# The experts' second weight matrices: loaded tile by tile into three buffers, in place of all eight kept in SBUF

## The chip, the cores and the metric

The kernel runs on one core of one Trainium2 chip. The metric is the device time of one execution in microseconds. The kernel is one launch: everything from the input x to the output is computed in it.

## What is computed

The reference is a small audio tower on x of shape (8, 128, 256): a token stage (smoothing in time and a projection to 256 features), attention, a mixture of experts, a second attention with a sigmoid-exponential weight, and a feed-forward layer with values rounded to eight bits. There are 8 x 256 = 2048 tokens of 256 features. The change concerns the mixture of experts, which is this:

```python
logits = x_flat @ gate_w.T + gate_b
probs = jax.nn.softmax(logits * ROUTE_SCALE, axis=-1)
topk_vals, topk_idx = jax.lax.top_k(probs, TOPK)          # TOPK = 2 of E = 8
dense_gate = jnp.zeros((N, E), probs.dtype).at[jnp.arange(N)[:, None], topk_idx].set(topk_vals)
h = jax.nn.relu(jnp.einsum('nd,edh->neh', x_flat, w1) + b1)     # w1: (8, 256, 1024)
y = jnp.einsum('neh,eho->neo', h, w2) + b2                      # w2: (8, 1024, 256)
out_flat = jnp.einsum('ne,neo->no', dense_gate, y)
```

Both weight matrices of one expert hold 1 MB each, in float32.

## The kernel before

The program is a row of blocks; within a block each engine has its own instruction list, written out by hand, and semaphores order the engines. The queues that matter are SP's, which issues nearly all DMAs in the order of its list and waits in that list, and PE's. Nothing is planned by a compiler: what stands behind a wait in SP's list is issued after it.

**First block (token stage, first attention, gate).** It works on the 8 batches in a software pipeline (`batches`, `iteration(b, u, k)`). For each batch SP issues twelve DMAs of 128 KB that spread parts of q and k over the partitions (`spread`, line 451), one small DMA (line 469) and the load of x of a later batch (line 400). Between them stand the loads of the eight second matrices (`load_w2`, line 436): experts 0, 4 and 5 at b = 0, experts 1 to 3 at b = 1 together with the biases (`load_b2`, line 440), and experts 6 and 7 after the last batch. They all go to `w2s`, 64 KB of each partition. GpSimd scatters each token's normalised row to the list `xg` in DRAM of each of its two experts. At the end of the block the kernel counts the tokens of each expert and makes a table `tile_e` with the expert of each of 39 tiles of 128 token slots, and `tile_row` with the tile's place in `xg`. SP then writes zeros behind the lists (line 385), and issues the first expert load `load_w1(sp, 0)` (line 370) and the first tile of rows `load_tile(sp, 0)` (line 376).

**Second block (experts, second attention).** `moe_tiles` runs `tile(i, u)` for i from -3 to 38 on every engine. In step i PE does the first layer of tile i+1 (line 1623), the transposes of the rows of tile i+2 (line 1637) and the second layer of tile i (line 1657). ACT and DVE each take half of the ReLU (lines 1248 and 1451), and DVE adds the bias and gives the result in `yt` (line 1458). SP in step i loads the rows of tile i+3 (line 376, two buffers `xt_in`) and its first matrix (line 370, three buffers `w1b`), then waits for `yt` of tile i and stores it to `yg` in DRAM (line 1142). Loads whose expert is known only at run time first read the table with `value_load`. PE also reads `tile_e`, once for each tile, to find the second matrix in `w2s`; it does so just ahead of the second layer.

Some steps carry work of the next stage: in steps 22 to 28 PE makes q, k and v of batch 0 of the second attention, and SP issues the twelve spreads of that batch (line 1128), three in step 26, three in 27, four in 28 and two in 29, each group right behind the store of `yt`. GpSimd gathers rows of `yg` back (`gather`, line 1188) once 16 tiles are stored, and again once 32 are.

The last block holds the feed-forward layer of the second half. The lists before the change, as far as the diff touches them:

Of the kernel before, what the change touches and what calls it, by code (L numbers as in the profile page):

```python
# [22 lines left out]
F32 = mybir.dt.float32  # L23
# [8 lines left out]
P = 128  # L32
# [64 lines left out]
def tower_kernel(nc, a, out):  # L97
    with ExitStack() as ctx:
# [72 lines left out]
        def carve(shape, dt, size):  # L171
            n = size
            for s in shape:
                n *= s
            start = used[0]
            used[0] = start + (n + 31) // 32 * 32
            assert used[0] <= ARENA, used[0]
            v = arena[:, start:start + n].bitcast(dt)
            if len(shape) == 2:
                v = v.rearrange("p (a b) -> p a b", a=shape[0])  # L180
            if len(shape) == 3:
                v = v.rearrange("p (a b c) -> p a b c", a=shape[0], b=shape[1])
            if len(shape) == 4:
                v = v.rearrange("p (a b c d) -> p a b c d", a=shape[0], b=shape[1], c=shape[2])
            return v


        b2r = carve([EXPERTS, D], F32, 4)
        w2s = carve([EXPERTS, HC, D], F32, 4)


        used[0] = B2_BYTES + W2_BYTES
# [130 lines left out]
            w8_in w8_step w8_mm w8_done q_step am_mm b_parts qz_q fT_mm fT_done f_mm f_o f_out""".split()  # L323
        scat = [sem(f"scat{u}") for u in range(2)]
        x_ld = [sem(f"x_ld{u}") for u in range(2)]
        w1_ld = [sem(f"w1_ld{n}") for n in range(W1_BUFS)]
        y_st = [sem(f"y_st{u}") for u in range(2)]
        o_out = [sem(f"o_out{u}") for u in range(2)]
# [28 lines left out]
        def batches(eng, iteration):  # L357

            for b in range(-2, 2):
                iteration(b, b % 2, b // 2)  # L360
            with eng.Fori(0, (B - 4) // 2) as it:
                for u in range(2):
                    iteration(it * 2 + (2 + u), u, it + 1)
            for b in range(B - 2, B + 2):
                iteration(b, b % 2, b // 2)

        def load_w1(sp, i):

# [24 lines left out]
        with nc.Block() as block:  # L393

            @block.sync
            def _(sp):
# [34 lines left out]
                            sp.dma_start(cols[:, i, j:j + 1], a[name][j * P:(j + 1) * P].rearrange("(h d o) -> d h o", h=HALVES, o=1)  # L431
                                         ).then_inc(S["w_in"], 16)

                def load_w2(e):

                    sp.dma_start(w2s[:, e], a["L0_ffn_w2"][e].rearrange("(c p) n -> p c n", p=P)).then_inc(S["w_exp"], 16)

                def load_b2():

                    sp.dma_start(b2r, a["L0_ffn_b2"].rearrange("(o e) d -> o e d", o=1).to_broadcast([P, EXPERTS, D])  # L440
# [13 lines left out]
                def iteration(b, u, k):  # L454
                    if stages(b + 2, 2, LAST):
                        load_x(b + 2, u, k + 1)
                    if isinstance(b, int) and b == 0:
                        load_w2(0)
                        load_w2(4)
                        load_w2(5)  # L460
                    if isinstance(b, int) and b == 1:
                        sp.wait_ge(S["wT_mm"], WT_STEPS)
                        for e in range(1, 4):
                            load_w2(e)
                        load_b2()
                    if stages(b, 0, LAST):

                        sp.wait_ge(S["mT_done"], b + 1)
                        sp.dma_start(stackq[SHIFT_ROW:SHIFT_ROW + 1, u], mT[0:HEADS, :]).then_inc(S["mrow"], 16)
                    if stages(b + 1, 0, LAST):  # L470
                        v = 1 - u
                        spread(b + 1, v, 0, 0, S["qh_done"], S["stk_q"])
                        spread(b + 1, v, 0, 1, S["kh_done"], S["stk_k"])
                        spread(b + 1, v, 1, 0, S["qm_done"], S["stk_q"])
                        spread(b + 1, v, 1, 1, S["km_done"], S["stk_k"])
                        spread(b + 1, v, 2, 0, S["ql_done"], S["stk_q"])
                        spread(b + 1, v, 2, 1, S["kl_done"], S["stk_k"])
# [2 lines left out]


                sp.wait_ge(S["xT_mm"], B)
                load_w2(6)
                sp.wait_ge(S["v_mm"], B)
                sp.wait_ge(S["stk_q"], 16 * SLOTS6 * B)
                sp.wait_ge(S["stk_k"], 16 * SLOTS6 * B)
                load_w2(7)
                zero_tails(sp, range(0, EXPERTS, 2))
                sp.wait_ge(S["p_step"], TILE_E_STEP)
                load_w1(sp, 0)  # L490
                sp.wait_ge(S["zfill"], 16 * (EXPERTS + 1))
                for u in range(2):
                    sp.wait_ge(scat[u], 16 + 16 * TOPK * QT * B // 2)
# [623 lines left out]
        with nc.Block() as block:  # L1117
            @block.sync
            def _(sp):
                def spread(b, u, part, which, done, landed):  # L1120

                    sp.wait_ge(done, b + 1)
                    if part == 0 and which == 0:
                        settled(sp)
                        wait(sp, S["s2_mm"], PAIRS * (b - 1))
                    stack = (stackq1, stackk1)[which]
                    for slot in (Q_SLOTS, K_SLOTS)[which][part]:
                        sp.dma_start(stack[u][DH * slot:DH * (slot + 1)].rearrange("d h t -> d (h t)"),
                                     n_qkp[which][:, part].rearrange("p j t -> p (j t)")).then_inc(landed, 16)

                def tile(i, u):
                    if i == 2:
                        sp.dma_start(w8, a["L1_ffn_weight"].rearrange("(j p) i -> p j i", p=P)).then_inc(S["w8_in"], 16)
                    v = 1 - u
                    if has(i + 3) and i + 3 >= 1:
                        wait(sp, S["tx_mm"], i + 2)
                        load_tile(sp, i + 3)
                        wait(sp, S["l1_hi"], i + 4 - W1_BUFS)
                        load_w1(sp, i + 3)
                    if has(i):  # L1140
                        sp.wait_ge(S["y_ev"], i + 1)
                        sp.dma_start(yg[i * P:(i + 1) * P, :], yt[:, u]).then_inc(y_st[u], 16)
                    if i == 26:
                        spread(0, 0, 0, 0, S["n_qh"], S["n_stkq"])
                    if i == 27:
                        spread(0, 0, 0, 1, S["n_kh"], S["n_stkk"])
                    if i == 28:
                        spread(0, 0, 1, 0, S["n_qm"], S["n_stkq"])
                        spread(0, 0, 1, 1, S["n_km"], S["n_stkk"])
                    if i == 29:  # L1150
                        spread(0, 0, 2, 0, S["n_ql"], S["n_stkq"])
                        spread(0, 0, 2, 1, S["n_kl"], S["n_stkk"])

                moe_tiles(tile)


                def iteration(b, u, k):
                    if stages(b + 1, 0, LAST):
                        spread(b + 1, 1 - u, 0, 0, S["n_qh"], S["n_stkq"])
                        spread(b + 1, 1 - u, 0, 1, S["n_kh"], S["n_stkk"])  # L1160
                        spread(b + 1, 1 - u, 1, 0, S["n_qm"], S["n_stkq"])
                        spread(b + 1, 1 - u, 1, 1, S["n_km"], S["n_stkk"])
                        spread(b + 1, 1 - u, 2, 0, S["n_ql"], S["n_stkq"])
                        spread(b + 1, 1 - u, 2, 1, S["n_kl"], S["n_stkk"])

                all_batches(iteration)
# [393 lines left out]
            def _(pe):  # L1560
# [69 lines left out]
                def tile(i, u):  # L1630
# [8 lines left out]
                    if has(i):  # L1639
                        if i == W8_TILE + 1:  # L1640
                            pe.wait_ge(S["w8_step"], 1)
                            pe.transpose(w8_am, w8s[:, 0:1].to_broadcast([P, P]), ident[:]).then_inc(S["w8_mm"], 1)
                        if i == W8_TILE + 4:
                            pe.wait_ge(S["w8_step"], W8_STEPS)
                            for c in range(DC):
                                for j in range(DC):
                                    mm = pe.transpose(w8_turn[:, c * D + j * P:c * D + (j + 1) * P],
                                                      w8q[:, j, c * P:(c + 1) * P], identb[:])
                            mm.then_inc(S["w8_mm"], 1)
                        if i == 0:  # L1650
                            pe.wait_ge(S["w_exp"], 16 * (EXPERTS + 1))
                        e = pe.value_load(tile_e[0:1, i:i + 1], min_val=0, max_val=EXPERTS - 1)
                        pe.wait_ge(S["reluA"], i + 1)
                        pe.wait_ge(S["reluD"], i + 1)
                        wait(pe, S["y_ev"], i)
                        for c in range(HC):
                            mm = pe.matmul(y_bank, hidT[:, u, c, :],  # L1657
                                           w2s[:, one(e), c, :].rearrange("p o n -> p (o n)"), start=(c == 0), stop=(c == HC - 1))
                        mm.then_inc(S["l2_mm"], 1)
                    if i == 22:  # L1660
                        turned_input(0)
# [226 lines left out]
```

## Time and profile before

| | us |
|---|---|
| median of 3 runs | 851.28 |
| lowest and highest | 846.99, 853.36 |
| the profiled execution | 855.8 |
| its span, first to last instruction | 854.0 |

The profile is that of one execution, on one core. Busy times are those of an engine's instructions; a matmul's end is modelled, and matmuls overlap their weight loads (PEld). The granted clock is TensorE's, as a share of full speed. The DMA share is the mean busy share of the core's 16 DMA engines and can pass 1 where packets overlap. "To landing" is the time from the issue of a DMA to the arrival of its last byte. A span cut into 40 slices gives 21.35 us for each. SP, ACT and POOL rows with a q are rows of that engine's DMA queue: when the instruction was issued, and for how long the issue took, not how long the data moved.

### The profile page before, as it was taken

To read this page: it belongs to the slowest core of one execution; us is meant where nothing else is said; L and a number is where in the kernel's file an instruction comes from. 1 tells how busy PE (TensorE), PEld (TensorE's weight loads), DVE (VectorE), ACT (ScalarE), POOL (GpSimd) and SP (SyncE) were. 2 spreads that over 40 slices of the span, in tenths; PEclk is the share of its full clock that TensorE was granted. 3 is DMA by queue.
4 is the path that set the end of the run, shared out by engine and by line. 5 is a ranking of instruction groups with operands and counts; after the bars stand their busy time and mean duration, and the time that the engine had idled before them with its cause. 6 is when DMAs were issued, how large, how long until landed. Compare 5 with 4: busy or idle time off the path is not lost. (4 is left out here: it accounts for less than half of the span.)

```text
span 854.0 us, 15973 instructions
## 1 busy us (share of the span) xinstructions
PE 730.1 (85%) x5604; PEld 580.3 (68%) x5604; DVE 447.0 (52%) x1111; ACT 349.9 (41%) x596; POOL 121.7 (14%) x166
## 2 busy tenths in 40 slices
PE   6488989889886299999999999998589888898646
PEld 5367767767664199999999999997366555664312
DVE  4536776776465222333223132231667888766677
ACT  3143345325432022222222132223687888988513
POOL 2010131232123300000010000101332223100000
PEclk9799999999999599999999999999798988998855
DMA  7989366346541555555565559740764466642002
GB/s 178 206 127 211 45 84 81 64 65 87 72 114 52 177 206 198 179 181 172 173 202 185 182 152 230 218 173 31 112 90 65 66 79 100 74 54 23 1 13 86
DMA packets 70710, 102.66 MB, mean 120 GB/s; under 512 B 8160, under 2 KB 58472, under 8 KB 70512
## 3 DMA queue, kind: packets, MB, share of 16 engines
q1 hardware_dynamic: 66928, 92.82, 49.0%
q0 software_dynamic: 3136, 8.40, 3.3%
q8 instruction: 42, 0.69, 0.4%
q10 hardware_dynamic: 576, 0.52, 0.2%
q14 instruction: 28, 0.23, 0.1%
HBM read 63.88 MB, written 12.58 MB: 90 GB/s over the span
## 5 line engine op out<-in xcount | busy, mean ns | idle before, releaser
L1623 PEld LDWEIGHTS psum<-arena 128*128 128x128 f32 x1248 | 147.1, 194 | 3.5 <-issue 1.7
L1623 PE MATMUL psum<-arena 128*128 128x128 f32 x1248 | 147.7, 277 | 1.1 <-ACT arena L1254 1.1
L1657 PE MATMUL psum<-arena 128*128 x624 | 141.3, 379 | 1.2 <-DVE arena L1458 1.2
L1657 PEld LDWEIGHTS psum<-arena 128*128 128x128 f32 x624 | 115.5, 190 | 15.7 <-issue 1.6
L1248 ACT ACTIVATE arena<-psum,arena 128x128 f32<-128x128 f32 x156 | 44.5, 368 | 197.4 <-PE psum L1623 140.3
L1585 PE MATMUL psum<-arena 96*128 96x256 bf16 x512 | 84.4, 299 | 26.3 <-ACT arena L1219 15.1
L1451 DVE TENSOR_SCALAR arena<-psum,arena 128x128 f32<-128x128 f32 x156 | 43.9, 344 | 94.7 <-PE psum L1623 75.2
L1585 PEld LDWEIGHTS psum<-arena 96*128 96x128 bf16 x512 | 47.1, 103 | 62.3 <-ACT arena L1219 26.9
L1343 DVE TENSOR_TENSOR arena<-arena 128x1024 f32<-128x1024 f32 x64 | 80.0, 1314 | 5.5 <-ACT arena L1218 3.1
L1219 ACT ACTIVATE arena<-psum,neg_mu 128x1024 f32<-128x1024 f32 x64 | 68.9, 1118 | 13.8 <-PE psum L1585 8.2
L1188 POOL DMA_INDIRECT w0T<-yg,pos x32 | 31.1, 971 | 301.0 <-DMA yg<-arena 239.3
L1458 DVE TENSOR_TENSOR arena<-psum,arena 128x256 f32<-128x256 f32 x39 | 16.6, 425 | 103.2 <-PE psum L1657 103.2
L762 DVE TENSOR_REDUCE arena<-psum 128x6 f32<-128x768 f32 x64 | 57.3, 951 | 21.0 <-PE psum L938 20.7
L1218 ACT ACTIVATE arena<-psum 128x1024 f32<-128x1024 f32 x64 | 63.1, 1030 | 8.5 <-PE psum L1585 8.1
L636 ACT ACTIVATE arena<-psum 128x768 f32<-128x768 f32 x64 | 48.6, 810 | 24.0 <-PE psum L955 23.5
L933 PE MATMUL psum<-arena 96*128 96x256 bf16 x128 | 37.5, 293 | 14.7 <-DMA arena<-arena 7.8
L1599 PE MATMUL psum<-arena 128*32 128x256 f32 x512 | 43.5, 470 | 0.3 <-DVE arena L1343 0.3
L950 PE MATMUL psum<-arena 97*128 97x256 bf16 x128 | 35.9, 280 | 4.2 <-ACT arena L636 4.2
L908 PE MATMUL psum<-arena,w0T 128*128 128x256 f32 x128 | 36.0, 445 | 1.8 <-ACT arena L607 1.1
L557 POOL DMA_INDIRECT xg<-arena,xslot x32 | 31.5, 985 | 22.4 <-DVE xslot L749 14.6
L908 PEld LDWEIGHTS psum<-arena,w0T 128*128 128x128 f32 x128 | 28.3, 226 | 7.1 <-issue 1.4
L534 POOL TENSOR_SCALAR veps<-mv 128x2 f32<-128x2 f32 x16 | 3.5, 219 | 204.7 <-DVE mv L685 204.7
(248 smaller groups left out, 1157.9 us busy)
## 6 DMA issues: line engine op xcount, KB each, us to landing
arena<-in_L_ffn_w_dram SPq DMA_DIRECT2D x47, 1024.0 KB, 5.4
arena<-arena SPq DMA_DIRECT2D x192, 128.0 KB, 6.0
arena<-xg SPq DMA_DIRECT2D x39, 128.0 KB, 2.0
yg<-arena SPq DMA_DIRECT2D x39, 128.0 KB, 1.7
out_dram<-arena SPq DMA_DIRECT2D x8, 256.0 KB, 2.1
arena<-in_x_dram SPq DMA_DIRECT2D x8, 128.0 KB, 7.3
arena<-in_L_ffn_b_dram SPq DMA_DIRECT2D x1, 1024.0 KB, 12.2
xg<-zeros SPq DMA_DIRECT2D x5, 128.0 KB
```

The source lines that it names most:

```text
L636: act.activation(probs[:, p], area[p % 2][:, :, 0:3 * P], ACT.Exp).then_inc(S["exp_done"], 1)
L762: dve.tensor_reduce(mx[:, 2 * p:2 * p + 2, :], area3[p % 3][:, :, 0:3 * P].rearrange("p i (n k) -> p i n k", k=P), AX, ALU.max).then_inc(S ...
L908: mm = pe.matmul(bank[:, j * T:(j + 1) * T], w0T[:, w, c, j * P:(j + 1) * P], xT[:, c, :], start=(c == 0), stop=(c == DC - 1))
L1218: return act.activation(out, in_, ACT.Exp)
L1219: return act.activation(out, in_, ACT.Sigmoid, bias=neg_mu[:])
L1248: ins = act.activation(hidT[:, v, c, :], psum[:, 2 * v, c * P:(c + 1) * P], ACT.Relu, bias=b1c[:, v, c:c + 1])
L1343: dve.tensor_tensor(first[:, u, p], first[:, u, p], second[:, p % 4], ALU.mult).then_inc(S["prodD"], 1)
L1451: ins = dve.tensor_scalar(hidT[:, v, c, :], psum[:, 2 * v + 1, (c - HALF) * P:(c - HALF + 1) * P], b1c[:, v, c:c + 1], 0.0, ALU.add, ALU.max)
L1585: mm = pe.matmul(area[p % 2][:, i, kt * T:(kt + 1) * T], stackk1[u][0:ROWS, hd, kt * P:(kt + 1) * P], stackq1[u][0:ROWS, hd, :], start=Tru ...
L1599: mm = pe.matmul(pv_out[32 * i:32 * i + 32, g], n_vaug[:, u, kt, head_of(4 * g + i), :], first[:, u, 2 * g + i // 2, i % 2, kt * T:(kt + 1 ...
L1623: mm = pe.matmul(psum[:, 2 * v + c // HALF, (c % HALF) * P:(c % HALF + 1) * P], w1b[:, i % W1_BUFS, d, c * P:(c + 1) * P], xtT[:, v, d, :] ...
L1657: mm = pe.matmul(y_bank, hidT[:, u, c, :], w2s[:, one(e), c, :].rearrange("p o n -> p (o n)"), start=(c == 0), stop=(c == HC - 1))
```

## The change

Each tile's second matrix is loaded from DRAM as its first one is. `w2s` with eight matrices becomes `w2b` with three (`W1_BUFS`), and a new `load_w2(sp, i)` reads `tile_e` and loads the 1 MB of tile i's expert into buffer i mod 3. Its place in SP's list: for tile 0 right behind `load_w1(sp, 0)`, for tiles 1 and 2 right behind their `load_w1`, and for tile i+3 behind the store of `yt` of tile i. In step 26 to 29 that is ahead of the spreads. The eight loads in the first block go away; the loads of the biases stay. PE's wait for all the second matrices becomes one for its buffer, and its `value_load` of `tile_e` and the address taken from it go away. Nothing else in SBUF moves: the other arrays keep their places.

```diff
-        w2s = carve([EXPERTS, HC, D], F32, 4)
+        w2b = carve([W1_BUFS, HC, D], F32, 4)
...
+        w2_ld = [sem(f"w2_ld{n}") for n in range(W1_BUFS)]
...
+        def load_w2(sp, i):
+
+            e = sp.value_load(tile_e[0:1, i:i + 1], min_val=0, max_val=EXPERTS - 1)
+            sp.dma_start(w2b[:, i % W1_BUFS], a["L0_ffn_w2"][one(e), :, :].rearrange("o (c p) n -> p (o c) n", p=P)
+                         ).then_inc(w2_ld[i % W1_BUFS], 16)
...
-                def load_w2(e):
-
-                    sp.dma_start(w2s[:, e], a["L0_ffn_w2"][e].rearrange("(c p) n -> p c n", p=P)).then_inc(S["w_exp"], 16)
-
...
-                    if isinstance(b, int) and b == 0:
-                        load_w2(0)
-                        load_w2(4)
-                        load_w2(5)
                     if isinstance(b, int) and b == 1:
                         sp.wait_ge(S["wT_mm"], WT_STEPS)
-                        for e in range(1, 4):
-                            load_w2(e)
                         load_b2()
...
                 sp.wait_ge(S["xT_mm"], B)
-                load_w2(6)
...
-                load_w2(7)
                 zero_tails(sp, range(0, EXPERTS, 2))
                 sp.wait_ge(S["p_step"], TILE_E_STEP)
                 load_w1(sp, 0)
+                load_w2(sp, 0)
...
                         load_w1(sp, i + 3)
+                        if i < 0:
+                            load_w2(sp, i + 3)
                     if has(i):
                         sp.wait_ge(S["y_ev"], i + 1)
                         sp.dma_start(yg[i * P:(i + 1) * P, :], yt[:, u]).then_inc(y_st[u], 16)
+                        if has(i + 3):
+                            load_w2(sp, i + 3)
...
                         if i == 0:
-                            pe.wait_ge(S["w_exp"], 16 * (EXPERTS + 1))
-                        e = pe.value_load(tile_e[0:1, i:i + 1], min_val=0, max_val=EXPERTS - 1)
+                            pe.wait_ge(S["w_exp"], 16)
+                        pe.wait_ge(w2_ld[i % W1_BUFS], 16 * (i // W1_BUFS + 1))
...
                             mm = pe.matmul(y_bank, hidT[:, u, c, :],
-                                           w2s[:, one(e), c, :].rearrange("p o n -> p (o n)"), start=(c == 0), stop=(c == HC - 1))
+                                           w2b[:, i % W1_BUFS, c, :], start=(c == 0), stop=(c == HC - 1))
```

## Rows read from the trace of the kernel before

**Rows 1.** The page's part 2 (40 slices), then the second layer's register instructions, line 1657.

```profile
PEclk9799999999999599999999999999798988998855
DMA  7989366346541555555565559740764466642002
...
L1657 PEldq FUSED_REGOPS  x312: 46/46/65, 307.9 to 588.5; - x156
```

**Rows 2.** A stretch: us, busy of PE, PEld, DVE, ACT, POOL, granted clock, DMA share, GB/s.

```profile
312.00:340.00 28.00, 28.00 (x197) 26.48 (x196) 7.74 (x29) 6.04 (x20) 0.00 (x0) 1.00 0.54 179
```

**Rows 3.** Timeline of the first tiles: start, us, engine, line, operation, idle before.

```profile
313.11 0.33 SPq L1142 DMA_DIRECT2D yg<-arena  x1
...
314.20 0.34 SPq L376 DMA_DIRECT2D arena<-xg  x1
...
315.31 0.38 SPq L370 DMA_DIRECT2D arena<-in_L_ffn_w_dram  x1
...
319.37 3.76 PEld L1623 LDWEIGHTS psum<-arena 128*128 128x128 f32 x32
...
323.05 0.25 PEld L1637 LDWEIGHTS psum<-ident,arena 128*128 128x128 f32 x2
...
323.27 3.32 PEld L1657 LDWEIGHTS psum<-arena 128*128 128x128 f32 x16
...
326.62 3.76 PEld L1623 LDWEIGHTS psum<-arena 128*128 128x128 f32 x32
```

**Rows 4.** SP's timeline, first three second-matrix loads; then a stretch in which they move.

```profile
25.63 7.02 SPq L436 DMA_DIRECT2D arena<-in_L_ffn_w_dram  x3
...
36.00:39.00 3.00, 2.88 (x37) 2.47 (x36) 3.00 (x4) 0.00 (x0) 0.00 (x0) 0.96 1.09 352
```

**Rows 5.** Stretches: spreads alone, a first matrix at its peak, the stage's start.

```profile
57.00:60.00 3.00, 2.76 (x45) 1.68 (x42) 0.00 (x0) 1.93 (x3) 0.00 (x0) 1.00 1.14 122
...
362.00:363.00 1.00, 1.00 (x6) 0.90 (x5) 0.00 (x0) 0.00 (x0) 0.00 (x0) 1.00 1.01 410
...
290.00:300.00 10.00, 2.13 (x9) 1.76 (x10) 1.00 (x3) 0.37 (x1) 0.81 (x1) 0.50 0.88 287
```

**Rows 6.** DMAs by line: 451 (the twelve from 17 to 26 us), 376, 370.

```profile
DMA to landing us min/median/max: 3.3/5.9/8.0
...
DMA to landing us min/median/max: 1.9/2.0/3.8
...
DMA to landing us min/median/max: 4.8/5.0/6.1
```

**Rows 7.** Timeline of the start of the expert stage, up to the first layer.

```profile
291.87 0.42 SPq L370 DMA_DIRECT2D arena<-in_L_ffn_w_dram  x1
293.52 1.87 SPq L376 DMA_DIRECT2D arena<-xg  x2
...
297.31 0.29 PEld L1637 LDWEIGHTS psum<-ident,arena 128*128 128x128 f32 x2 [10.64 <-DMA arena<-xg]
...
298.56 5.70 PE L1623 MATMUL psum<-arena 128*128 128x128 f32 x32 [0.55 <-ACT arena L1254]
```

**Rows 8.** Timelines of SP (stores 26 to 29) and PEld (transposes of tiles 32, 33).

```profile
505.76 0.33 SPq L1142 DMA_DIRECT2D yg<-arena  x1
...
513.00 0.34 SPq L1142 DMA_DIRECT2D yg<-arena  x1
...
521.97 0.34 SPq L1142 DMA_DIRECT2D yg<-arena  x1
...
529.22 0.34 SPq L1142 DMA_DIRECT2D yg<-arena  x1
...
531.91 0.26 PEld L1637 LDWEIGHTS psum<-ident,arena 128*128 128x128 f32 x2
...
539.16 0.25 PEld L1637 LDWEIGHTS psum<-ident,arena 128*128 128x128 f32 x2
```

**Rows 9.** PE's waits between 10 and 75 us: us in total, times, longest.

```profile
PE psum L933 <- DMA arena<-arena: 7.3, 2, 5.0
```

## The prediction

> **What bounds the kernel now.** I read the page first, for where the stages lie: in its DMA line the experts are the eleven fives and sixes from the fourteenth slice on and the 9, 7 and 4 behind them, with TensorE's clock at 9 in all but the first of these slices [rows 1]. Then I cut that stage into stretches. From 312 to 340 us PE is busy for 28.00 of 28.00 us at a granted clock of 1.00, while the DMA engines are at 0.54 [rows 2]. So PE alone sets the end of this stage, and the DMA engines have room. The timeline gives the rhythm: the first layer of one tile starts at 319.37 and that of the next at 326.62, so a tile takes 7.25 us, made of 3.7 us first layer, 0.2 us transposes and 3.35 us second layer, back to back [rows 3]. ACT, DVE and GpSimd have slack. The change touches what runs beside PE. Its question is whether the DMA engines can carry twice the weights without making PE wait.
>
> **Removed: eight loads in the first block.** The first three are issued at 25.63 us [rows 4]. PE does wait there for spreads, 7.3 us in two waits [rows 9], but these spreads were issued ahead of the loads, and twelve of them land up to 8.0 us after issue by their own bulk [rows 6]: they move at 122 GB/s with the DMA engines at 1.14 and nothing beside them [rows 5]. The loads move behind them, at 352 GB/s, while PE and DVE are busy [rows 4]. I cost the removal at 0. Bounds: no loss has a mechanism; the gain is at most the 7.3 us of those waits, were the loads their cause, and I take 0 since the order of issue rules it out.
>
> **Removed: PE's table read and address arithmetic.** The second layer has 312 register instructions of 46 ns, 8 in each tile, 0.37 us [rows 1], and a read of the table, which has no row of its own. PE's sequencer does both ahead of the array, which never runs dry [rows 2]. Cost 0; what it would be without that cover is the first rival.
>
> **Added: one load of 1 MB in each tile.** I need the time that each transfer takes of the shared DMA engines when they queue. A second matrix: 1.049 MB at 352 GB/s is 3.0 us [rows 4]. A first matrix: its peak is 410 GB/s [rows 5], 2.6 us; its landing of 5.0 us less the 1.6 us that a small load of rows has beyond its own 0.4 (2.0 us in all) is 3.4 us [rows 6], but that has a ramp which a queue would hide. I take 2.8, with 2.45 and 3.2 as the ends. Rows and result are 0.131 MB each, 0.4 us. The sum is 3.0 + 2.8 + 0.4 + 0.4 = 6.6 us in a tile of 7.25 us, the DMA engines 91% loaded. So in a plain tile they keep up. The shares say the same: 0.54 x 7.25 = 3.9 now [rows 2], plus 3.0 x 1.09 = 3.3 [rows 4], is 7.2, against the 7.9 that a tile offers at the 1.09 of a full queue: 91%.
>
> Is each transfer in time? Take tile 0's store at 313.11. The new load goes out 1.1 us behind it (the distance from one table-addressed issue to the next, 314.20 to 315.31 [rows 3]) and holds the matrix of tile 3, whose second layer starts a tile behind the one at 323.27 [rows 3], so at 330.5: 17 us for a transfer that needs 4.6. But behind it in SP's list stand the rows of tile 4, needed by the transposes at 323.05, and its first matrix, needed at 326.62 [rows 3]. They go out 1.1 us later and queue behind the 3.0 us. Counted from the store: the second matrix lands at 1.1 + 1.6 + 3.0 = 5.7 us, the rows at 6.1, the first matrix at 8.9, against limits of 9.9 and 13.5. So a plain tile has 3.8 us to spare, and the chain is done before the next burst has to land. Cost 0. All the same the margin is small, and the steps that put more into the queue use it up.
>
> A rule of the Trainium skill speaks against this (DMA: Bandwidth & Descriptors, Measured (HBM→SBUF, 128 partitions, SWDGE, issued from GpSimd) and the formula in Anatomy of one DMA): a DMA costs about 2.0 us fixed plus its bytes at 436 GB/s. If the fixed part occupied the engines, an estimate from that page for four transfers of 2.36 MB would be 13.4 us for a tile, and the stage would nearly double. The three loads issued together, which moved at 352 GB/s [rows 4], say that the fixed parts overlap.
>
> **The start of the stage: +3.0 us.** The load of tile 0's first matrix goes out at 291.87, its rows at 293.52, and PE starts on the rows at 297.31 having waited 10.64 us for them [rows 7]. That is 3.8 us from issue to landing, against a median of 2.0 [rows 6]: the rows lie behind the first matrix. Now 1.049 MB more lie between the two. SP's extra 1.1 us is hidden, since the matrix ahead still moves. So the rows land 3.0 us later, and first layer and all behind it move by that, the slow first 4 us of PE at half clock included (5.70 us for the first layer [rows 7]). Nothing covers it: PE has nothing else. Tiles 1 and 2 follow in the queue in time. By the same prices the first matrix of tile 1 lands near 303.6, and tile 0's first layer ends at 298.56 + 5.70 + 3.0 = 307.3; the rows of tile 2 land near 306.7, and are wanted a first layer later, at 311.0. Bounds: 0, if the queues let the rows pass, and 4.1, if SP's 1.1 us adds.
>
> **The spreads in steps 26 to 29: +5.4 us.** Twelve spreads of 0.131 MB at 122 GB/s are 1.07 us each [rows 5]. Three, three, four and two of them now stand between second matrix and rows. The stores go out at 505.76, 513.00, 521.97 and 529.22 us; of the four transposes that want the rows behind them the last two start at 531.91 and 539.16 [rows 8], the two before at 7.25 and 14.5 us less than the first of these, 524.66 and 517.41. Burst 26: second matrix out at 506.86, landed 511.5, spreads 514.7, rows 515.1, first matrix 517.9. Burst 27 queues behind it: 0.4 + 3.0 + 3.2 + 0.4 gives rows at 524.9, 0.2 late; first matrix 527.7. Burst 28, with four spreads: rows at 535.8, wanted at 532.1, 3.6 late; first matrix 538.6. Burst 29: rows at 544.5, wanted at 539.16 + 3.85 = 543.0, 1.5 late. Burst 30 has no spreads: rows at 551.1, wanted at 546.4 + 5.4 = 551.8. The sum of lateness is 5.4 us. With first matrices of 2.45 us it is 3.9, with 3.2 us (where GpSimd's second gather adds 1.0 later) 7.5. Below, nothing, if the limits leave more than I see. PE waits for these rows ahead of the second layer of the same step, so a late row delays everything behind. The later blocks only move.
>
> **Sum.** 0 + 0 + 0 + 3.0 + 5.4 = +8.4 us. On the profiled execution, 855.8 us, that is 864.2. That execution lies 4.5 us above the median of the runs, 851.3, so I forecast 851.3 + 8.4 = 859.7 us for the median. What a few runs can tell from no change is about 1%, 8.5 us: the forecast sits on that border.
>
> **Rivals.**
> *PE's sequencer is the limit (faster than before).* If the 0.37 us of address arithmetic and the table read, by the nearest row the 0.77 us in SP's list between the end of one issue and the next (314.54 to 315.31 [rows 3]), set the tile's 7.25 us, dropping them gives back up to 39 x 1.14 = 44.5 us, and 851.3 + 8.4 - 44.5 = 815.2 us. It decides once the plain tile's period falls by more than 8.4 / 39 = 0.22 us. For it speaks only that they stand in PE's list ahead of the second layer; against it, PE's 28.00 busy of 28.00 [rows 2].
> *The spreads fit in (little change).* If the transfers overlap better than my prices, so that four spreads, a second matrix and rows land in 10 us, only the start is left: 851.3 + 3 = 854.3, up to 856. For it: at present the same steps pass without a wait on PE.
> *The DMA engines saturate (clearly slower).* If reads and writes mixed move at the 287 GB/s of the stretch from 290 to 300 us [rows 5], and not at my 358, a tile needs 2.36 / 0.287 = 8.2 us, and some 35 tiles lose 1.0 us each. With 13 us of spreads laid bare and 3 at the start that is +51, 902 us. It decides at 7.25 us for a tile, or 326 GB/s; the second matrices alone beat that [rows 4], and the 287 holds gaps between issues.
> *Fixed costs add up* (the page's formula as above). By rows, if each of four DMAs held the engines for the 1.6 us beyond its bytes [rows 6], a tile would take 6.6 + 6.4 = 13.0 us, +5.75 us x 39, 1076 us. Against it stands the rate in [rows 4].
>
> **Chances.** Forecast (start and spreads, +5 to +12, 856 to 863.5 us): 0.60. Spreads fit in: 0.21. Saturation in any degree, from +12 up: 0.14. Sequencer, faster: 0.04. Fixed costs: 0.01. Slower by over 1% is half of the first case, 0.30, with 0.15 of saturation and fixed costs, so 0.45; faster is the sequencer's 0.04; the rest, 0.51, is within 1%. The range from 853 to 870 takes in most of the case of the spreads that fit and the mild part of saturation, and leaves out some 0.15: the sequencer, full saturation and the fixed costs.
>
> **What would show it.** Right: PE waits in the profile after for the rows (line 1637) once at the start, some 13.5 us in place of 10.6, and again near 535 and 543 us by 1 to 4 us each; plain tiles keep 7.25 us; no wait at line 1657 for the new buffer; DMA share near 0.9 to 1.0 from 312 to 580 us; the first block's line 1009 and the table at the same times as before. Wrong: a tile period above 7.25 us in the plain stretch from 312 to 500 us (saturation), below it (sequencer), waits of line 1623 for first matrices ahead of any for rows, or a first block that ends earlier.

## The result, and the profile after

The changed kernel takes 861.2 us (median of 4 runs, 860.36 to 862.67) where the kernel before takes 849.87 in the same comparison (846.99 to 853.36). The ratio is 1.0133, with a 95% interval of 1.0089 to 1.0177: slower by 11.3 us, clear of the noise, though a little over 1% of the time. The profiled execution took 860.36 us, with a span of 858.6.

From the page's part 2 of the kernel after, in 40 slices of 21.5 us (it answers to [rows 1]), and two stretches with the columns of [rows 2]:

```profile
PEclk9799999999997599999999999999799888998855
DMA  7584366545601989999999899992764456642002
...
312.00:340.00 28.00, 28.00 (x197) 26.48 (x196) 8.72 (x32) 5.00 (x17) 0.00 (x0) 1.00 0.96 334
500.00:550.00 50.00, 42.19 (x291) 39.16 (x290) 11.35 (x37) 9.24 (x30) 0.00 (x0) 1.00 0.98 273
```

The stage's fives have become nines. PE is still busy for 28.00 of 28.00 us in the plain tiles, as in [rows 2], with the DMA engines at 0.96 in place of 0.54. Between 500 and 550 us PE is idle for 7.8 us. The waits of PE's weight loads in the stage (total, times, longest), then the start and the late rows in the timeline:

```profile
PEld psum L1637 <- DMA arena<-xg: 22.8, 5, 14.2
...
277.59 3.93 SPq L392 DMA_DIRECT2D xg<-zeros  x4
282.39 0.41 SPq L377 DMA_DIRECT2D arena<-in_L_ffn_w_dram  x1
283.65 0.40 SPq L371 DMA_DIRECT2D arena<-in_L_ffn_w_dram  x1
284.96 1.80 SPq L383 DMA_DIRECT2D arena<-xg  x2
...
291.90 0.29 PEld L1637 LDWEIGHTS psum<-ident,arena 128*128 128x128 f32 x2 [14.21 <-DMA arena<-xg]
...
310.33 0.25 PEld L1637 LDWEIGHTS psum<-ident,arena 128*128 128x128 f32 x2
317.57 0.26 PEld L1637 LDWEIGHTS psum<-ident,arena 128*128 128x128 f32 x2
...
513.88 0.20 PEld L1637 LDWEIGHTS psum<-ident,arena 128*128 128x128 f32 x2 [1.85 <-DMA arena<-xg]
523.06 0.20 PEld L1637 LDWEIGHTS psum<-ident,arena 128*128 128x128 f32 x2 [1.89 <-DMA arena<-xg]
533.80 0.20 PEld L1637 LDWEIGHTS psum<-ident,arena 128*128 128x128 f32 x2 [3.45 <-DMA arena<-xg]
542.46 0.20 PEld L1637 LDWEIGHTS psum<-ident,arena 128*128 128x128 f32 x2 [1.38 <-DMA arena<-xg]
```

(Line 377 loads a first matrix now, 371 a second, 383 rows, 1140 stores, 1124 spreads.) All five waits of PE on a transfer are for rows of tokens. One is at the start: the rows are issued behind the second matrix, and PE waited 14.21 us for them where it had waited 10.64 [rows 7]. Four are at the steps with spreads, 8.57 us together. Plain tiles are 7.24 us apart (310.33 to 317.57), as before.

To compare many profiles I cut each into four lengths: the first block up to the first zero DMA; from there to PE's first transposes of rows (**start**); from there to PE's first transposes of the second attention, line 1564 (**stage**); and the **rest** of the span. This table is worked out from the timelines. The last column names the comparison that a profile belongs to. Comparisons 2, 3 and 4 ran on three different chips; which one comparison 1 ran on isn't on record. The kernel before took 849.9 us in comparison 1, 858.5 in 2, 858.1 in 3 and 847.9 in 4.

| kernel | first zero DMA | start | stage | rest | comparison |
|---|---|---|---|---|---|
| before | 286.46 | 10.85 | 293.79 | 262.9 | 1 |
| before_b | 276.27 | 10.70 | 293.83 | 263.7 | 4 |
| before_c | 280.49 | 10.58 | 293.36 | 262.4 | 4 |
| before_d | 281.24 | 10.52 | 293.42 | 262.4 | 4 |
| after | 277.59 | 14.31 | 302.32 | 264.4 | 1 |
| again (the same) | 288.49 | 13.58 | 301.60 | 267.3 | 3 |
| early | 288.80 | 13.86 | 302.25 | 269.6 | 2 |
| start | 289.85 | 10.58 | 301.71 | 266.2 | 2 |
| late | 285.26 | 13.67 | 298.16 | 267.6 | 2 |
| both | 288.95 | 10.86 | 298.11 | 264.7 | 2 |
| actq | 288.05 | 14.37 | 296.50 | 262.6 | 3 |
| thin | 290.52 | 10.50 | 293.87 | 267.0 | 3 |
| thin_early | 277.58 | 11.35 | 294.80 | 264.6 | 4 |

Start and stage hardly scatter. The four profiles of the kernel before have 10.66 and 293.60 us in the mean; the three with the change as it was made (after, again, early) have 13.92 and 302.06. So the change costs 3.3 us at the start and 8.5 us in the stage, 11.7 us in all. First block and rest scatter by several us for the same code, and the first block more from comparison to comparison. TensorE's clock goes along with that: the 2151 or 2152 recorded matmuls of the first block keep PE busy for 222.5 us at a granted clock of 0.94 in "after", and for 228.8 and 230.2 us at 0.92 in "before" and "again".

The two lengths don't explain every total. In the eight variants below that were run several times, the time over the kernel before of the same comparison is 1.0 to 3.8 us more than start and stage are longer than 10.66 and 293.60 ("early" and "again" are the ends). Comparisons 2 and 3 have no profile of the kernel before, so this can't be placed; in comparison 4 the rest is 264.6 us with the change and 262.4 to 263.7 without. A small loss outside start and stage is not excluded.

### The profile page after: what moved, and what is told of

Same layout as the page of the kernel before. It is cut to its first block and busy times, and to the rows that moved or that the text cites. A ratio compares the mean times of both kernels' runs of the same rounds, so it can differ in the third digit from the quotient of the medians.

```text
span 858.6 us, 15810 instructions
## 1 busy us (share of the span) xinstructions
PE 725.5 (85%) x5604; PEld 576.7 (67%) x5604; DVE 446.7 (52%) x1111; ACT 349.8 (41%) x596; POOL 122.0 (14%) x166
## 5 line engine op out<-in xcount | busy, mean ns | idle before, releaser
L1657 PE MATMUL psum<-arena 128*128 128x256 f32 x624 | 141.3, 379 | 1.1 <-DVE arena L1458 1.1
L1254 ACT COPY arena<-psum 128x256 f32<-128x256 f32 x39 | 14.6, 374 | 52.8 <-PE psum L1637 52.6
L904 PE MATMUL psum<-arena,w0T 128*128 128x256 f32 x128 | 33.0, 416 | 1.8 <-ACT arena L603 1.1
L1637 PE MATMUL psum<-ident,arena 128*128 128x128 f32 x78 | 15.4, 280 | 21.9 <-DMA arena<-xg 21.9
```

Of the source, the lines that this page charges most:

```text
L1657: mm = pe.matmul(y_bank, hidT[:, u, c, :], w2b[:, i % W1_BUFS, c, :], start=(c == 0), stop=(c == HC - 1))
```

## The experiments

**Theory.** Nearly all transfers of the stage go through one queue in the order of SP's list, and the engines behind it are nearly full. PE loses time where rows of tokens, which it needs at once, stand behind a second matrix: once at the start, and in steps 28 to 31, where the spreads fill what room there was. **Rivals.** The loss is contention that no order cures; or part of the difference sits in the first block, whose length differed by 8.9 us between the first two profiles.

### The start alone

```diff
                 load_w1(sp, 0)
-                load_w2(sp, 0)
...
                 load_tile(sp, 0)
+                load_w2(sp, 0)
```

> The changed kernel with one line moved: the second matrix of tile 0 is issued behind the rows of tile 0, not ahead of them. Theory (the rows queue behind 1 MB more, +3.0 us forecast; in the two profiles the distance from the first zero DMA to PE's first transposes of rows went from 10.85 to 14.31 us, +3.46): the distance falls back to about 10.9 us, and the time by 3.5 us, from 861.2 to about 857.7. Rival (the start is late for another reason, such as SP's longer list): the distance stays above 13 us and the time at 861.

Measured: 869.52 us (6 runs), 1.0140 of the kernel before (1.0110 to 1.0171). The profile shows what was moved:

```profile
289.85 3.83 SPq L392 DMA_DIRECT2D xg<-zeros  x4
...
300.43 0.29 PEld L1637 LDWEIGHTS psum<-ident,arena 128*128 128x128 f32 x2 [10.50 <-DMA arena<-xg]
```

The start is back at 10.58 us, the length of the kernel before, and the stage is unchanged at 301.71. In the total the gain of 3.3 us, 0.4%, can't be told: the kernels with the change as made had 1.0133, 1.0141 and 1.0167, with intervals of about 0.004 either way. The lengths settle that the order at the start costs 3.3 us ("both" and "thin", with the same move, have 10.86 and 10.50 us too); the total doesn't contradict it, and doesn't show it.

### The second matrix behind rows and first matrix

```diff
                         if i < 0:
                             load_w2(sp, i + 3)
+                    if i >= 1 and has(i + 2):
+                        load_w2(sp, i + 2)
...
-                        if has(i + 3):
-                            load_w2(sp, i + 3)
```

> The changed kernel with the second matrix of tile i+3 issued one transfer later in steps 0 on: behind the rows and the first matrix of tile i+4, not ahead of them. Theory (one first-in-first-out chain of transfers; PE waits for the rows of tiles 30 to 33 by 1.85 + 1.89 + 3.45 + 1.38 = 8.57 us because the chain is full in steps 26 to 29): every row is wanted with the same work ahead of it but one matrix of 3.0 us, so the sum of the waits falls by 3.0 to about 5.6 us and the time to about 858.2. Rival (each row is late by the one matrix right ahead of it, 3.0 us each): the waits of all but the third vanish, under 1 us is left, and the time falls by 8, to 853. No second layer waits for its matrix in either.

Measured: 867.16 us (6 runs), 1.0112 (1.0074 to 1.0150). The stage fell from 302.06 to 298.16 us, by 3.9, where one matrix of 3.0 was expected, and not by 8. The waits fell to a single one, of 2.61 us, under the 5.6 us I had written and over the rival's 1 us. The stage shows less waiting than lost time. The transposes of two tiles in the timeline, and two stretches, one of them in the tile between:

```profile
536.40 0.20 PEld L1637 LDWEIGHTS psum<-ident,arena 128*128 128x128 f32 x2 [2.61 <-DMA arena<-xg]
545.29 0.25 PEld L1637 LDWEIGHTS psum<-ident,arena 128*128 128x128 f32 x2
...
536.74 5.25 PE L1657 MATMUL psum<-arena 128*128 128x256 f32 x16
...
534.00:535.00 1.00, 0.00 (x0) 0.00 (x0) 0.92 (x4) 0.00 (x0) 0.00 (x0) 1.00 1.06 355
538.00:539.00 1.00, 1.00 (x4) 0.79 (x3) 0.00 (x0) 0.00 (x0) 0.00 (x0) 0.50 1.07 347
```

PE stands idle until 536.40 us for rows. Then the granted clock is 0.50, the 1.2 GHz level, for some 3 us, and the second layer that falls into them takes 5.25 us in place of 3.6. The next transposes come 8.89 us later, not 7.25: 1.64 us lost with no wait beside them. Wait and slow clock are 4.25 us, near the 4.6 by which this stage is above 293.60. In the kernel after, four waits of up to 3.45 us left the clock at 1.00. My 5.6 us came from the 8.57 us of the kernel after. The two profiles of the same comparison that have the stage as the change made it, "start" and "early", have 5.69 and 5.04 us of waits for rows. Against them the waits fell by 2.4 to 3.1 us, the theory's 3.0; against the kernel after, by 6.0. With one profile of each, the stage's length, 3.9 us shorter, is the better witness, and it too is near the theory's 3.0 and far from the rival's 8.

### Both moves together

The edits are the two above in one kernel.

> Both moves together. Theory: the parts add, 861.2 - 3.5 - 3.0 = 854.7 us, with 5.6 us of waits for rows left in steps 28 to 31. If the second move takes away all 8.6: 849. If the start's gain is given back in the wait for spreads: 858.

Measured: 864.45 us (9 runs), 1.0070 (1.0044 to 1.0096). Start 10.86 us, stage 298.11: the parts add, as the theory has it. The wait that is left is one of 3.03 us at the rows of the same tile as in "late", with 0.26 us of wait at the next one, and in between again a tile of 8.86 us with the granted clock at half.

### The early loads put back

```diff
-        w2b = carve([W1_BUFS, HC, D], F32, 4)
+        w2s = carve([EXPERTS, HC, D], F32, 4)
+        w2b = w2s[:, 0:W1_BUFS]
...
+                def load_early(e):
+
+                    sp.dma_start(w2s[:, e], a["L0_ffn_w2"][e].rearrange("(c p) n -> p c n", p=P)).then_inc(S["w_exp"], 16)
...
+                    if isinstance(b, int) and b == 0:
+                        load_early(0)
+                        load_early(4)
+                        load_early(5)
```

The other five stand at their old places too.

> The changed kernel, and in its first block the eight loads of the kernel before again, at their old places in SP's list and into the same bytes of SBUF (nobody reads them; the three buffers lie on the first three of them, so SP waits for the eight ahead of the first load of a tile). Theory (the removal is worth nothing, since those loads queue behind the spreads that PE waits for): the same time as the changed kernel, 861 us, within 2. Rival (in the two profiles the first zero DMA came at 286.46 us before and at 277.59 after, 8.9 us earlier, and the missing loads are the reason): 870 us, with that DMA near 286.

Measured: 871.34 us (6 runs), 1.0141 (1.0109 to 1.0173), between the 1.0133 and 1.0167 of the same kernel without these loads. The first zero DMA came at 288.80 us, and at 285.26, 288.95 and 289.85 in the three kernels of the same comparison without them. The waits for spreads in the first block (PE, 10 to 75 us; line numbers moved), first in the kernel after, then here:

```profile
PE psum L929 <- DMA arena<-arena: 8.1, 2, 5.4
```

```profile
PE psum L943 <- DMA arena<-arena: 6.7, 2, 5.1
```

They are no longer with the loads than without, and [rows 9] has 7.3. The loads didn't cause them. The rival's figures, 870 us with that DMA near 286, look close to what came, 871.34 and 288.80, but only because the chip was slower: against the 849.9 us of the first comparison 870 is 1.024, and 1.0141 was measured. The removal is worth nothing that these runs can tell, which is to within about 3 us.

### The changed kernel once more

No edit.

> The changed kernel as it is, timed with the others and a second profile taken. Theory: 1.013 times the kernel before, as the first time; start of the stage 14.3 us from the first zero DMA to PE's first transposes, waits for rows of 5 to 9 us in steps 28 to 31. The first block's own length is expected to differ by several us from that of the first profile, since four kernels with the same first block had their first zero DMA at 277.6, 285.3, 289.0 and 289.9 us.

Measured: 872.84 us (6 runs), 1.0167 (1.0138 to 1.0196). Start 13.58, stage 301.60 us. The first zero DMA was at 288.49, 10.9 us later than in the first profile of this same kernel. Its waits in steps 28 to 31 were two, of 1.24 and 4.31 us, and a tile of 8.89 us behind the second: fewer waits and a slow clock in place of four waits at full clock, and nearly the same stage. PE's waits between 500 and 560 us in "early", "again" and "start", three profiles with the stage as the change made it, and a stretch of "again" behind its longer wait:

```profile
PEld psum L1651 <- DMA arena<-xg: 5.0, 2, 2.9
...
PEld psum L1637 <- DMA arena<-xg: 5.6, 2, 4.3
...
PEld psum L1637 <- DMA arena<-xg: 5.7, 2, 4.7
...
543.00:547.00 4.00, 4.00 (x13) 3.34 (x14) 0.00 (x0) 0.37 (x1) 0.00 (x0) 0.64 1.12 316
```

Set out by the four groups of spreads, worked out from the timelines (the last column is the length of each such tile less 7.25 us and less any wait in it):

| | waits behind steps 26, 27, 28, 29 | sum | lost in tiles at half clock |
|---|---|---|---|
| forecast (parts rounded) | 0, 0.2, 3.6, 1.5 | 5.4 | none |
| after | 1.85, 1.89, 3.45, 1.38 | 8.57 | none |
| again | 0, 1.24, 4.31, 0 | 5.55 | 1.64 |
| start | 0, 0.97, 4.72, 0 | 5.69 | 1.62 |
| early | 0, 2.12, 2.92, 0 | 5.04 | 1.73 and 1.40 |

"Start" has one more wait, of 0.3 us, for a first matrix. The kernel after, from which I had read the loss, is the odd one of the four.

### The spreads handed out over twelve steps

To both moves this adds:

```diff
-                    if i == 26:
-                        spread(0, 0, 0, 0, S["n_qh"], S["n_stkq"])
...
+                    if 26 <= i < 26 + 2 * SLOTS6:
+                        part, which, slot, done = thin[i - 26]
+                        sp.wait_ge(S[done], 1)
+                        sp.dma_start((stackq1, stackk1)[which][0][DH * slot:DH * (slot + 1)].rearrange("d h t -> d (h t)"),
+                                     n_qkp[which][:, part].rearrange("p j t -> p (j t)")
+                                     ).then_inc(S[("n_stkq", "n_stkk")[which]], 16)
```

`thin` lists the same twelve transfers in the same order; the other three groups go as the first does.

> Both moves (tile 0's second matrix behind its rows; the others behind the rows and first matrix of the next tile), and the twelve spreads of steps 26 to 29 handed out one for each step from 26 to 37, in the same order. Theory (what is left of the loss, 1.007 times the kernel before with both moves, is the full chain in steps 26 to 29, 2.6 to 3.0 us of waiting for rows and 1.6 us of half clock behind it): each step now adds 1.07 us of spread to 6.6 us of transfers, 0.4 us over the tile's 7.25, twelve times, 5 us, of which a plain tile's slack covers 3.8 and the longer step 27 1.7: no wait for rows, and the time within 0.3% of the kernel before. Rival (the loss is contention that placing does not cure): 1.005 or more.

Measured: 860.81 us (12 runs), 1.0032 (1.0010 to 1.0053). PE's waits on transfers in the stage are the one at the start, and the transposes in question come at the pace of plain tiles:

```profile
PE psum L1635 <- DMA arena<-xg: 10.3, 1, 10.3
...
528.44 0.25 PEld L1635 LDWEIGHTS psum<-ident,arena 128*128 128x128 f32 x2
535.68 0.25 PEld L1635 LDWEIGHTS psum<-ident,arena 128*128 128x128 f32 x2
542.93 0.25 PEld L1635 LDWEIGHTS psum<-ident,arena 128*128 128x128 f32 x2
```

Start and stage are 10.50 and 293.87 us, those of the kernel before (10.66 and 293.60), with twice the weights still moving. That is against contention: placing alone cures the whole loss in the stage. The total alone could not say so, since the interval reaches the rival's 1.005. The kernel does not beat the one before: the interval's lower end is above 1.

### The second matrices on ACT's queue

```diff
                         act.copy(xtT[:, u].rearrange("p c t -> p (c t)"), x_bank).then_inc(S["xtT_done"], 1)
+                    if i >= 1 and has(i + 2):
+                        load_w2(act, i + 2)
```

SP's loads of tiles 3 on go away.

> The changed kernel with the second matrices of tiles 3 on issued by ACT, on ACT's DMA queue, behind its copy of the transposed rows (in step i that of tile i+2); those of tiles 0 to 2 stay with SP. Theory (the loss comes from the order in one queue and the full engines): rows no longer lie behind the matrix of the same step but share the engines with it, so the waits for rows in steps 28 to 31 fall to about 4 us, and the time to 1.009 of the kernel before; the start keeps its 3.5 us. Rival (two queues give no order, so the big transfers slow the small ones in every tile): rows land later in plain tiles too, and the time is above 1.015.

Measured: 867.09 us (4 runs), 1.0115 (1.0083 to 1.0147). Start 14.37 us, unchanged; stage 296.50, so 5.6 us less than with the change as made, and less than "late" by 1.7. One wait for rows is left, of 1.44 us, and waits under 1 us for matrices. I had written 4 us of waits. The theory's 1.009 is within the interval; the rival's 1.015 lies just outside it. Two queues do spread the time over all: a second matrix lands 8.2 us after issue (median, 320 to 500 us) against 7.1 in the kernel after, while rows land in 4.3 against 6.3, where the rival had them later.

### A third matrix in each step

```diff
                         if has(i + 3):
                             load_w2(sp, i + 3)
+                            n = i % W1_BUFS
+                            sp.wait_ge(w2x_ld[n], w2x_had[n] + 16 * (i // W1_BUFS))
+                            sp.dma_start(w2x[:, n], a["L0_ffn_w2"][i % EXPERTS].rearrange("(c p) n -> p c n", p=P)
+                                         ).then_inc(w2x_ld[n], 16)
```

> The changed kernel with a third load of 1 MB in each step (a second matrix, in 1 KB runs, into bytes that nobody reads), right behind the second matrix. It measures what the transfers of a tile cost of the DMA engines when these are the limit. Theory (3.0 us for a second matrix, 2.8 for a first, 0.4 each for rows and result): a plain tile takes 9.6 us in place of 7.25, 3.41 MB at 355 GB/s, and the stage some 36 x 2.35 = 85 us longer. Rival (mixed traffic moves at 287 GB/s): 11.9 us for a tile.

Measured: 948.83 us (one run); the stage took 376.5 us, 82.7 more than 293.8, where 85 was expected. Two of its transposes, seven tiles apart, and a stretch:

```profile
369.27 0.20 PEld L1648 LDWEIGHTS psum<-ident,arena 128*128 128x128 f32 x2 [1.88 <-DMA arena<-xg]
...
434.00 0.20 PEld L1648 LDWEIGHTS psum<-ident,arena 128*128 128x128 f32 x2 [1.82 <-DMA arena<-xg]
...
340.00:500.00 160.00, 130.55 (x855) 119.31 (x855) 37.42 (x127) 26.25 (x86) 3.85 (x4) 0.98 1.07 370
```

A tile takes 64.73 / 7 = 9.25 us, for 3.41 MB: 369 GB/s, 370 in the stretch. At that rate the 2.36 MB of a tile of the changed kernel need 6.4 us. My 6.6 was right to within 0.2 us, and the rival's 287 GB/s wrong: the engines are loaded to 88% in a plain tile, and don't set its length.

### The kernel before, three more times

No edit.

> The kernel before as it is, profiled again, to see its own lengths on such a chip as the experiments ran on: first zero DMA, PE's first transposes of rows, end of the stage. Theory (the removal of the early loads is worth nothing, and the 8.9 us between the first two profiles was scatter): the first zero DMA comes near 288 us, within the 285.3 to 290.5 of the kernels without those loads; the start takes 10.85 us and the stage 293.8. Rival (the removal changes the first block): outside of that band.

> The kernel before once more, for the scatter of one kernel on one chip. Theory: first zero DMA between 285 and 291 us. Rival: outside.

> The kernel before a third time, for the same scatter. Theory: first zero DMA between 285 and 291 us. Rival: outside.

Measured: 846.31, 848.65 and 849.45 us, with the first zero DMA at 276.27, 280.49 and 281.24 us, all outside the band that I wrote down. Read by the words on record, these are three hits for the rival. But this was another chip than those of the band, a faster one (the kernel before took 847.9 there against 858.1 to 858.5), so they don't test it: the miss is in comparing across chips. What did come as written is start and stage, 10.70 and 293.83 us in the first of the three. What they show is scatter: 5.0 us between three executions of one kernel on one chip. The kernel after, at 277.59, and the first profile before, at 286.46, lie 8.9 apart; the kernel after again was at 288.49. With start and stage within 0.5 us of one another in all four profiles of before, the first block is where executions differ.

### The early loads put back into the best order

The edits of "thin" and of "early" in one kernel; SP waits for the eight ahead of the first load into the buffers:

```diff
                 load_tile(sp, 0)
+                sp.wait_ge(S["w_exp"], 16 * (EXPERTS + 1))
                 load_w2(sp, 0)
```

> The kernel with both moves and the spreads handed out, and the eight early loads put back as in the kernel before (read by nobody). It measured 1.0032 of the kernel before without them, with the stage itself at 293.87 us against 293.79. Theory (the early loads are worth nothing; the 0.3% left is scatter or lies elsewhere): again 1.003. Rival A (their absence makes the first block longer): 1.000. Rival B (their absence had made it shorter, which hides a loss elsewhere): 1.006 or more.

Measured: 850.97 us (12 runs), 1.0036 (1.0010 to 1.0062), with the first zero DMA at 277.58 us, between the before's 276.27 and 281.24 on that chip. The same as without the loads, 1.0032: neither rival. Stage 294.80, with 1.0 us of waits in the stage beside that of the start. The 0.3% over the kernel before stays in both, and I can't place it: here start and stage make 1.9 of the 3.0 us, in "thin" 0.1 of 2.7. Both intervals exclude 1, so noise of the totals is an unlikely reason; in single profiles such small amounts drown in the scatter of first block and rest.

## Why the prediction came out as it did

The forecast was 859.7 us, +8.4; measured were 861.2, +11.3, within the range of 853 to 870. That the two times lie only 1.5 us apart is in part luck: the difference was 2.9 us more than forecast, and the kernel before took 849.9 us in that comparison and not the 851.3 that I added to. By steps:

- **The early loads, 0.** Right. The profile after showed a first block 8.9 us shorter, which I had named as a sign against me. The loads put back changed nothing that could be told, twice, and the same code scattered by 10.9 us from comparison to comparison and 5.0 us on one chip.
- **PE's table read and arithmetic, 0.** Right. Plain tiles are 7.24 us apart with and without them. The first rival, a faster kernel, falls.
- **Throughput of the engines, 6.6 us a tile.** Right by the run with a third matrix, 6.4. The third rival falls. So does the fourth, fixed costs that add up: four transfers of a plain tile fit in 7.24 us where it had 13.0, and five in 9.25. The Trainium skill gives a DMA issued from GpSimd a fixed cost of about 2.0 us (DMA: Bandwidth & Descriptors, Anatomy of one DMA). Four times that is 8.0 us, more than the whole tile, so in these traces, with DMAs issued from SP, such costs overlap.
- **The start, +3.0 us.** Right: 3.3 us, removed by moving one line.
- **The spreads, +5.4 us.** The mechanism was right: the loss in the stage is rows waiting behind matrices and spreads, with a slow clock behind some of the waits, and placing cured it. The size was low: 8.5 us, outside even the 7.5 I had as upper end. The second rival, that the spreads fit in, falls.

This last term was mis-sized in two ways, and which of them shows differs by profile. In "again", "start" and "early" the waits for rows are 5.0 to 5.7 us, what I had forecast, and near it step by step. What was missing is the clock: the tiles behind a wait ran at half clock for part of their length and cost 1.6 us more, in "early" 3.1 us for two of them. I had counted the slow clock at the start of the stage and put it at nothing here, without a reason. In the kernel after the clock stayed at 1.00 and the waits themselves were 8.57 us.

For those waits the step that failed is the one on landing in time. I wrote that rows would land 6.1 us behind the store of their burst and the first matrix at 8.9, by 1.6 us beyond the bytes ahead, with 3.8 us to spare. The landing rows of the kernel after, between 320 and 500 us, for the lines 1140, 371, 383 and 377:

```profile
DMA to landing us min/median/max: 2.9/4.3/5.2
...
DMA to landing us min/median/max: 6.2/7.1/7.9
...
DMA to landing us min/median/max: 5.4/6.3/7.1
...
DMA to landing us min/median/max: 6.9/7.9/8.6
```

Each is above what I had by empty-queue rows: the store 4.3 us against 2.0, the second matrix 7.1 against 4.6. Rows, issued about 2.3 us behind the store, land 8.6 behind it, and the first matrix, 3.4 behind it, at 11.3: 2.4 later than I had it. Against the limit of 9.9 the rows had 1.3 us to spare, not 3.8. The 1.6 us came from transfers that met an empty queue [rows 6]; with one that is 88% full a transfer also waits for what is left of the tile before, at every tile, though the engines keep up over the whole tile. The landings show it: the first matrix lands 11.3 us behind the store of its burst, so 4.1 us behind the next store, and that store lands at 4.3. With less to spare, the first two of the four bursts, which I had at 0 and 0.2 us late, were late by 1.85 and 1.89. In "again" the same medians are 3.9, 6.6, 5.7 and 7.2 us, which leaves the rows 1.9 us to spare, and there the first burst was in time. That the difference of 0.6 us decided it is likely, and not shown.

A second part was not in my chain at all. The order of issue in step 26:

```profile
500.28 0.34 SPq L1140 DMA_DIRECT2D yg<-arena  x1
...
501.37 0.49 SPq L371 DMA_DIRECT2D arena<-in_L_ffn_w_dram  x1
502.00 2.63 SPq L1124 DMA_DIRECT2D arena<-arena  x3
505.40 0.35 SPq L383 DMA_DIRECT2D arena<-xg  x1
...
509.05 5.52 SPq L1124 DMA_DIRECT2D arena<-arena  x3
```

The three spreads of the next step take SP 5.52 us to issue, where three took 1.87 to 1.92 in the kernel before, and no wait stands between them in SP's list. SP is held at the issue, and with it the rows. It is so in the other profiles with a second matrix right ahead of the spreads (in "again" 2.94, 4.76 and 5.35 us for the last three groups), and not in "late", where the matrix goes out earlier, ahead of the store (1.84, 2.59 and 1.22). That a full queue is what holds SP fits this, but no run shows it by itself. And the second matrix issued at 501.37 landed 10.4 us later, against 7.1 in plain tiles, though the spreads were issued behind it. My chain had what is issued later never delay what is issued earlier. How much of the 3.2 us of waits beyond my 5.4 in the kernel after is this and how much the shorter spare time, I haven't separated.

## What to carry to other kernels

A stream of large loads that fits its engines on average can still cost time, by what stands behind it in the queue: look for the small transfer that an engine waits for at once, and issue the large one, which has tiles of time, behind it. Take the spare time of each transfer from rows at the load that the queue will have, since landing times from an empty queue promise too much, and hand extra traffic out over steps when it is near 90%. Give a wait in the middle of full work a term for the slow clock behind it too. Read a loss of this size from more than one profile: here four of the same stage split it differently. A kernel's executions can scatter in a block that the change never touched; compare the lengths between marks in several profiles before a difference there is called an effect.

## What the runs showed of the hardware

Waits of PE of 2.1 to 4.7 us in the middle of full work were followed in "late", "both", "start", "again" and, twice, in "early" by a tile of 8.6 to 9.0 us, waits left out, in place of 7.25. In "late" the rows show the granted clock at 0.50, the 1.2 GHz level, for about 3 us behind the wait; in "again" it is 0.64 over the 4 us behind it. Waits of up to 3.45 us in the kernel after, and of 1.24 us and 1.44 us in "again" and "actq", were followed by no fall, so the length of the wait alone doesn't tell. Where the clock fell, the price was 1.4 to 1.7 us more than the length of the wait. And the DMA engines sustained 370 GB/s of mixed traffic in 1 KB and longer runs over 160 us, above the 352 that second matrices alone had shown [rows 4].
